# The weight ring of an output projection, from two slots to four

## The reference

```
Q, K, V = x @ W_Q, x @ W_K, x @ W_V        # plus low-rank terms for K, V of tiers 0 and 1
attn = softmax(causal(Q K^T / 8));  head_out = attn V          # 24 heads
x = layernorm(x + concat(head_out) @ W_O)
h = silu(x @ w_gate) * (x @ w_up)
h = keep the 2 largest of each 4 by absolute value
x = layernorm(x + h @ w_down)
```

## Time and profile before

| | us |
|---|---|
| timed runs of the kernel before | 6301.05 and 6231.2, median 6266.13 |
| profiled execution, slowest core | 5790.29 |
| its span (first to last instruction), core 2 | 5788.8 |
| spans of the other cores | 5743.6 to 5785.1 |

### The profile page before, as it was taken

One profiled execution on the slowest core, in us unless ns is written; L12 is line 12 of the kernel. 1 busy time (PEld: TensorE's weight loads), 2 busy tenths in 40 slices (PEclk: granted clock), 3 DMA queues, 4 the chain that ended last, 5 costly groups with the idle time before them and its releaser, 6 DMA issues.

```text
span 5788.8 us, 61600 instructions; the slowest of 8 cores (5743.6 to 5788.8 us)
## 1 busy us (share of the span) xinstructions
PE 4743.2 (82%) x20400; PEld 1848.6 (32%) x20400; DVE 1839.8 (32%) x2803; ACT 1149.9 (20%) x1205; POOL 435.9 (8%) x800
## 2 busy tenths in 40 slices
PE   0578889776757876886899999899994899979994
PEld 0233334221111211221344444344441344434441
DVE  0111212444433323223345454200055445440004
ACT  0000000344727836882000000000000000000000
POOL 0000000000000000000000000122200000002220
PEclk9989999877878887887999999899996999989996
DMA  9532333322122131111455555799852455549992
GB/s 153 77 59 48 65 61 75 95 76 77 59 99 59 56 124 46 59 66 59 80 96 95 94 102 88 154 216 215 173 95 70 91 95 95 95 91 213 218 220 88
DMA packets 360620, 592.60 MB, mean 102 GB/s; under 512 B 85504, under 2 KB 208576, under 8 KB 357056
## 3 DMA queue, kind: packets, MB, share of 16 engines
q0 software_dynamic: 155968, 260.75, 30.2%
q1 hardware_dynamic: 204352, 327.92, 18.0%
HBM read 767.26 MB, written 88.28 MB: 148 GB/s over the span
## 4 chain that ended last, share of the span: by engine, by line
PE 62%; DVE 13%; DMA 10%; ACT 6%; issue 5%; another core or an unknown queue 3%; DVEq 0%; ACTq 0%; SPq 0%; POOLq 0%; POOL 0%
PE ps L748 15%; PE ps L758 15%; PE ps L875 14%; DMA vspill<-ar 6%; ACT ar L545 5%; PE ps L348 4%; PE ps L576 4%; DVE ar L557 4%; PE ps L522 2%; DMA ar<-wospill 2%; PE ps L441 2%; PE ps L683 1%; PE ps L986 1%; DMA ar<-wd 1%
## 5 line engine op out<-in xcount | busy, mean ns | idle before, releaser
L748 PE MATMUL ps<-ar 128*128 128x512 bf16 x4096 | 1220.8, 380 | 62.5 <-DMA ar<-wg 32.2
L758 PE MATMUL ps<-ar 128*128 128x512 bf16 x4096 | 1220.5, 380 | 1.0 <-DMA ar<-wu 1.0
L875 PE MATMUL ps<-ar 128*128 128x512 bf16 x4096 | 907.2, 383 | 82.4 <-DMA ar<-hspill 57.9
L545 ACT ACTIVATE ar<-ps 128x1024 bf16<-128x1024 f32 x960 | 905.2, 1067 | 274.7 <-PE ps L530 265.5
L576 PE MATMUL ps<-ar 128*65 128x512 bf16 x1920 | 660.3, 437 | 31.7 <-DVE ar L557 31.1
L522 PE MATMUL ps<-ar 64*128 64x512 bf16 x960 | 395.2, 428 | 259.6 <-ACT ar L545 165.6
L875 PEld LDWEIGHTS ps<-ar 128*128 128x128 bf16 x4096 | 401.3, 98 | 588.3 <-issue 125.9
L748 PEld LDWEIGHTS ps<-ar 128*128 128x128 bf16 x4096 | 401.1, 98 | 548.8 <-issue 67.4
L758 PEld LDWEIGHTS ps<-ar 128*128 128x128 bf16 x4096 | 401.2, 98 | 486.5 <-issue 4.6
L778 ACT ACTIVATE ar<-ps 128x1024 bf16<-128x1024 f32 x128 | 131.1, 1024 | 2105.8 <-PE ps L748 1469.6
L557 DVE TENSOR_TENSOR ar<-ar 128x512 bf16<-128x512 bf16 x768 | 313.5, 425 | 513.8 <-ACT ar L545 470.4
(11 more groups left out here) (101 smaller groups left out, 2656.5 us busy)
## 6 DMA issues: line engine op xcount, KB each, us to landing
ar<-hspill SPq DMA_DIRECT2D x512, 256.0 KB, 5.8
ar<-wg POOLq DMA_DIRECT2D x128, 512.0 KB, 6.2
ar<-wu POOLq DMA_DIRECT2D x128, 512.0 KB, 8.8
ar<-wd POOLq DMA_DIRECT2D x512, 128.0 KB, 6.3
ar<-wospill SPq DMA_DIRECT2D x72, 512.0 KB, 3.6
hspill<-ar SPq DMA_DIRECT2D x128, 256.0 KB, 6.7
ar<-xT POOLq DMA_DIRECT2D x8, 2048.0 KB, 21.2
ar<-xTo POOLq DMA_DIRECT2D x8, 2048.0 KB, 15.8
```

What stands on the lines that cost most here:

```text
L545: lambda e, b0=b0, eap=eap: e.activation(eap, ps[:, b0 * 512:(b0 + 2) * 512], AF.Exp, scale=0.125),
L748: lambda e, bb=bb, th=th, kc=kc, s=s, wgs=wgs: e.matmul(bank(bb + th), wgs[:, kc * 128:(kc + 1) * 128], x1[:, kc * 2048 + s * 512: kc * 20 ...
L758: lambda e, bb=bb, th=th, kc=kc, s=s, wus=wus: e.matmul(bank(bb + 2 + th), wus[:, kc * 128:(kc + 1) * 128], x1[:, kc * 2048 + s * 512: kc ...
L875: lambda e, bi=bi, ft=ft, th=th, ic=ic, wst=wst, hst=hst: e.matmul(bank(bi), wst[:, ft * 128:(ft + 1) * 128], hst[:, th * 512:(th + 1) * 512],
```

## The change

The ring of the projection gets four slots in place of two, with two more semaphores, and the wait for outstanding loads at the end of phase B names them too. The slot is `ho % 4` in each group.

```diff
     for s in ("sp", "sv", "sa", "xb0", "xb1", "xos", "wkv",
-              "wr0", "wr1", "wr2", "wr3", "or0", "or1", "wql", "k0", "k1", "v0", "v1", "mk", "ql",
+              "wr0", "wr1", "wr2", "wr3", "or0", "or1", "or2", "or3", "wql", "k0", "k1", "v0", "v1", "mk", "ql",
@@
             nho = 6 if grp == 0 else HPN
             for ho in range(nho):
-                rsl = ho % 2
+                rsl = ho % 4
                 rB = B["ring"][rsl]
                 wst = A(ring_o + rsl * 2048, 2048)
                 evl = dma("sync", "or%d" % rsl, wst, wospill[ho],
@@
     kb.raw_wait("sync", [(n, kb.cnt[n]) for n in ("k0", "k1", "v0", "v1", "mk",
-                                                   "ql", "or0", "or1")])
+                                                   "ql", "or0", "or1", "or2", "or3")])
```

## The result

| | before | after |
|---|---|---|
| timed runs, median | 6156.8 us (16 runs) | 5772.0 us (17 runs) |
| lowest run | 5783.3 us | 5722.5 us |
| ratio, of the runs named below | | 0.9897, 95% interval 0.9868 to 0.9926 |
| the four projections, mean over the 8 cores (lowest and highest core) | 208.9 us (201.4 to 217.8) | 147.9 us (144.5 to 157.7) |
| first score to first gate matmul, mean over the cores | 1673.9 us | 1613.9 us |

One thing must be known to read the medians: in 11 of the 16 timed runs of before and 8 of the 17 of after the four cores of one die, or all eight, are granted a lower clock and the run takes 2 to 11% longer, and both runs of before that stand ahead of the prediction (6231.2 and 6301.05) were such runs; the ratio leaves them out.

The account below looks back on a forecast made before the run. TensorE was taken as busy for most of the span, the projections bound by load landings. Per strip 6.1 + 5.2 + 2.6 + 20.7 = 34.6 us, with additions 37; 70 or 64 us less, taken as 66: 6266 - 66 = 6200, range 6130 to 6275.

Parts of the forecast that it names:

- The base: Whole kernel: start from the two timed runs' median, 6266 us, and subtract 66 to get 6200.
- My correction from 70 to 64 us: Projections in timed runs: if the 8.2% longer time stretches matmuls alone, the saving is 64 us instead of 70.
- The saving: Four output projections: 37 us a strip, 148 in all against 217.7, so 70 us less in the profiled execution.
- The border: Between a projection's two groups: VectorE's additions set the 5.37 us, the new tile's load fits inside; 2.6 us lost, as before.
- Load 5: Group 0 of a projection: issued at 6.1 us, wanted at 10.0, so 3.9 us to land, just enough.
- What is late next: After the projection: eight additions and the layer norm move earlier unchanged in length, so each us saved stays saved.
- A: Ring loads: the rate does not rise, a tile still costs 2.7 us; 31 us less, 6235; chance 0.11.
- B: Ring loads: the deeper ring slows its own loads; at 3.7 us a tile, 21 us more, 6287; chance 0.02.
- C: TensorE in the projections: the clock stays at 0.50 throughout, 22 us more; chance 0.02.
- D: Whole kernel: a larger gain; four projections give at most 79 us, over 2% only from run spread; chance 0.05.
- The clock: Projection matmuls: by the skill's rule alone no clock fall is left, 76 us less; the forecast kept one, 1.6 us a strip.
- The transfer size: Ring loads: the skill asks for 1 MiB a transfer; by that rule more 512 KB slots buy little, as in A.

Follow-up runs that it names:

- the bank-by-bank kernel: Eight half slots, with the last four tiles of each group multiplied block by block instead of tile by tile; four projections 127.6 us, against 142.7.
- the running count: Changed kernel, its four slots taken by a count running over groups and strips instead of `ho % 4`; four projections 143.1 us, against 147.9.
- the half loads: Kernel before, still two slots, each load bringing only its group's 1024 columns (256 KB); four projections 20.9 us less, ratio 0.9961.
- Eight half slots: Changed kernel with eight 256 KB slots in the room of four, taken by a running count; four projections 142.7 us, against 147.9.

## Why the prediction was right about the change and wrong about the time

**The base: wrong.** The step that failed is the one from the profiled execution to the runs: "476 us (8.2%) more, and no row says where", and then 6266 - 66. I took the two runs as the kernel's time and the profiled 5790 as the exception. It is the other way round: of the 16 runs of before five lie at 5783 to 5813, and the profiled execution, 5790, was such a one. Had I subtracted 60 to 70 from the execution that I had in rows, I would have said 5720 to 5730; the lowest run was 5722, the profiled one 5744. The text said that it did not know where the 476 us were and still built its range upon them; the range should have held both bases.

**What the 476 us are: seen in another kernel.** No trace was kept of the two runs of before. But the profile of the three-slot kernel is of an execution of 6338.7 us, in which cores 0 to 3 were granted a lower clock. These are the same 700 us of the feed-forward part on core 3 and on core 6:

```profile
2900.00:3600.00 700.00, 700.00 (x2712) 292.06 (x2710) 278.74 (x322) 43.01 (x42) 50.93 (x84) 0.83 0.41 80
...
2900.00:3600.00 700.00, 700.00 (x3245) 317.32 (x3244) 334.48 (x385) 52.18 (x51) 54.38 (x102) 1.00 0.53 95
```

Core 3 did 2712 matmuls where core 6 did 3245, at a granted clock of 0.83 for 1.00. Its feed-forward part took 3426.8 us against 2905.7, its strips 1658.9 against 1633.3, its four projections 167.9 against 170.6. So the loss lies almost wholly where TensorE runs dense, and none of it in the projection. That the 476 us of before are the same loss is argued from this; why the clock is lower in some executions is open. My correction from 70 to 64 us "if matmuls alone are stretched" had no object. That it moved the number towards the measured 60 is luck.

**The saving: right mechanism, one term too large.** 37 us a projection was predicted, 37.0 is the mean after. The landing time of 4.5 us (4.6), the additions of 4.67 us at the border (4.67 in core 2, strip 3) and 250 to 300 GB/s (311 in strip 0, 235 in strip 3) came. Mis-sized was the term of before: 217.7 us was the sum of core 2, the slowest core and nearly the worst of the eight at this; the mean is 208.9. So the saving is 61 and not 70. A slowest core is slow in part by what is about to be removed, and its own sum does not carry over to the next execution, whose slowest core is another.

That the 37 fits so well is luck in part, since two of its parts are off and cancel. From tile 5 to tile 1 of group 1 pass 6.4 us in place of 5.6 (next paragraph). The eleven tiles behind take 20.2 us in place of 21.2 (19.0 + 0.6 for wait instructions + 1.6 for a fall of the clock): the fall comes in 16 of 32 projections and not in each, and the bank-by-bank kernel runs through at 0.216 us a matmul, so nothing is seen of the 0.05 us a tile.

**The border: wrong.** "The load of the new tile takes 3.2 to 3.7 us from the end of tile 4, which is inside that", inside VectorE's 5.37 us, compares two things that end at different matmuls. The last bank is wanted by the eighth matmul of the new tile, the load by the first, and 0.35 us of start and the eight matmuls, 1.73 us, still come behind the landing: 0.1 + 3.2 + 0.35 + 1.73 = 5.4 us from the end of tile 4, level with VectorE at best. The landings there were 3.1 to 4.7 us. So the load, and not VectorE, sets the start of group 1 in each of the 32 projections, and makes the border 0.75 us longer than VectorE alone would; the idle time "<- DVE" in the timeline hid that. The price is small, 3 us in the four projections, and the running count takes it back.

**Load 5: nearly right.** "Just enough" holds for most projections. Cores 5 and 6 needed 40 to 42 us in strips 0 and 1, with late loads inside the groups as well, as on core 5 (0.16, 0.53 and 2.36 us behind `wospill`, besides the 3.47 of the border):

```profile
1253.85 1.46 PE L683 MATMUL ps<-ar 128*128 128x512 bf16 x6 [0.16 <-DMA ar<-wospill]
1258.78 10.51 PE L683 MATMUL ps<-ar 128*128 128x512 bf16 x40 [3.47 <-DMA ar<-wospill]
1269.83 10.52 PE L683 MATMUL ps<-ar 128*128 128x512 bf16 x48 [0.53 <-DMA ar<-wospill]
1282.70 3.04 PE L683 MATMUL ps<-ar 128*128 128x512 bf16 x8 [2.36 <-DMA ar<-wospill]
```

Why these two cores see later loads than the others was not settled.

**What is late next: right.** The phase around the projections shrank by 60.0 of 61.0 us.

**The rivals.** A is refuted by the half loads and by the gain itself; what is true in it is that landings grow with the depth (3.3, 3.6, 4.6 us for one, two and three or four slots). B did not come: 311 GB/s. C did not come: 1.00 in the run of group 1, but for the stretch of some 3.4 us that half of the projections have. D was right in that four projections can't give 2%.

**The two rules.** The clock: TensorE: Matmul & The Clock Gate, of the Trainium skill, section HAM oscillation, puts the fall down to waits for loads inside the loop, and the prediction took from it that none would be left. The changed kernel is no test of that, since its load at the border is still late; it has a fall in 16 of 32 projections. Eight half slots are the test: no load is late, and 24 of 32 have a fall, behind the stretch in which VectorE frees the banks 0.8 us apart. With that stretch gone too, none of 32 has one (32.36 us for 136 matmuls). So a wait for another engine does it as well as one for a load; but with the running count the same stretch has a fall behind it in 1 of 32 alone, and what decides between 1 and 24 is open. The one slot shows the full price, 3.27 us for eight matmuls in place of 1.9. The transfer size: DMA: Bandwidth & Descriptors, section Rules for kernel authors, asks for 1 MiB or more; here 512 KB loads, four deep, moved 311 GB/s, and 256 KB loads, eight deep, left TensorE no wait for a load at all. In this stage, with loads queued deep enough, size was not what mattered.

## What to carry to other kernels

Where the chain of waits alternates between a load's landing and its use and never passes from load to load, the cost of a tile is (landing + use) / slots: add slots until that falls below the engine's own time, and take the landing as somewhat longer at each depth. When the ring no longer binds, look at what stood beside it: here the bank-wise additions, which an order of matmuls bank by bank hid, gave another 35 us of 1609. Where two waits end at one place, ask which instruction each of them holds up, and check the releaser that a view names against the landing: the load held up the first matmul, the additions only later ones. And before a forecast is anchored on timed runs, set them beside the profiled execution: where they differ by 8% and no row explains it, the range has to hold both.

## What the hardware showed that was not expected

A ring of one slot cost more than its waits: 67 us more a projection than two slots, of which some 23 us (13 tiles at 3.27 for 1.90 us, 4 of six matmuls at 2.7 for 1.46) is TensorE at a lower clock. The reverse came too, though not everywhere: with no gap left in the projection, the layer norm's single-row matmuls behind it, which have a gap of 0.46 us before every second one, ran at 1.00 in strip 0, where they had run at 0.50, and that was worth 3 us; in the other strips the clock fell (0.57 in strip 1), and it was worth 0.5. And a landing of 512 KB is, by the estimate above, only half due to its bytes: 3.6 us, and 2.7 us for half of them.
